# W4 and the two weights of the last layer as split operands in float32r, in a four-layer graph network on one core

## The chip, the cores and the metric

The kernel runs on one core of a Trainium2 chip. The metric is the device time of one execution in microseconds (us). Engines: TensorE (PE; PEld is its weight load), VectorE (DVE), ScalarE (ACT), GpSimd (POOL) and SyncE (SP, which issues most DMAs).

## The reference

128 nodes with 512 features, 4096 edges (src, dst) with 64 features each. Four layers follow each other, and after each x = layernorm(x + layer(x)):

```
L0: attention over the edges' adjacency, then a feed-forward part (not touched by the change)
L1: h   = mish([x[src], x[dst], edge_attr] @ W1 + b1)        # 4096 x 512
    agg = segment_sum(mish(h @ W2 + b2), dst)                # 128 x 512
    u   = mish([x, agg] @ W3 + b3)
    out = layernorm(x + u @ W4 + b4) * gamma + beta
L2: two graph convolutions, 512 -> 128 -> 512
L3: h   = x @ W_self.T + mean_of_neighbours(x) @ W_neigh.T + bias
    out = layernorm(h) * gamma + beta
```

## The kernel before

Everything is on chip after the first load. A float32 matmul of the source appears in the trace as two PE instructions (two passes), each with a weight load of its own; a float32r matmul is one. Where float32r is used, an operand v is split: hi = float32r(v), lo = v - hi, and the product is the sum of three matmuls, hi*hi + hi*lo + lo*hi. Before the change that holds for W1 and W2 of L1 and for the edge tensors; W3, W4 and all that comes after them are float32.

**The loop.** L1's edges go in G = 8 groups g of 512, each of 4 tiles t of 128. PE's order in group g is written out (lines 705 to 717): second_layer(g, 0), first_layer(g+1, 0), sum_messages(g-1), first_layer(g+1, 1), second_layer(g, 1), first_layer(g+1, 2 and 3), second_layer(g, 2 and 3). In the last group, g = 7, the first_layer parts are absent. sum_messages (671) adds the messages of tile t to bank 0 with two matmuls, from Mhi (678) and Mlo (679), and waits before each tile for `m_lo` of that tile. For each tile DVE adds the bias to the bank (z2_out, 994), ACT takes mish twice, to Mhi (380) and to M (381), and DVE subtracts (message_low, 999). DVE's order (1019 to 1041) and ACT's (388 to 400) are written out as well; each engine works in order, so an instruction put into either list delays all that stand after it. On DVE a group ends with one_hot (1006), z2_out 2, message_low 2, z2_out 3, message_low 3.

**The tail.** After the loop PE runs the last sum, W3 (update, 719; matmuls in line 472) and W4 (741, matmuls in line 463: banks 2 and 4 each take half of the 512 columns, K in four chunks c). ACT turns W3's banks into uT (404), DVE adds the residual (823) and normalises. PE then multiplies by ones (748), turns W_self and W_neigh by transposes (turn, 683, eight calls; ACT copies each out in line 408 to WsT, chunks 0 to 3, and WnT), transposes y (754; ACT copies xT in 415), and does L2: 760, DVE's r0 (1058, 1066), 767, ACT's r1g (418), 770, ACT's p1g (420), 776, and DVE's statistics (816) and norm (841). For L3 it transposes xs, forms the neighbours' mean (783, bank 2), and multiplies by WsT and WnT (788, 791), all in line 463. DVE copies xT (1075) and nmT (1077), adds beta (1079) and takes the statistics of banks 4 and 0 (1080).

**SP** loads W3, W4, W_self and W_neigh during the loop, each behind a count of finished second_layer tiles (246 to 253).

```
for t in ts:                                     # sum_messages, PE
    pe.wait_ge(S["m_lo"], GT * g + t + 1)
    mm(AGG[:, :], Dg[:, t, :], Mhi[:, t, :], start=g == 0 and t == 0, stop=False)
    done = mm(AGG[:, :], Dg[:, t, :], Mlo[:, t, :], start=False, stop=g == G - 1 and t == GT - 1)
```

Of the kernel before, what the change touches and what calls it, by code (L numbers as in the profile page):

```python
# [40 lines left out]
def gnn_kernel(nc, a, out):  # L41

    ctx = ExitStack()
    with ctx:
# [36 lines left out]
        def overlay(*spots):  # L81

            made = {}
            with ExitStack() as st:
                end = 0
                for name, place, units, dt in sorted(spots, key=lambda s: s[1]):
                    if place > end:
# [14 lines left out]
        low = overlay(("Clo", 0, 32, F32R), ("Mlo", 64, 4, F32R))  # L102
        last = overlay(("W3", 0, 8, F32), ("W4", 8, 4, F32), ("WsR", 12, 4, F32), ("WnR", 16, 4, F32),
                       ("WsT", 32, 4, F32), ("WnT", 36, 4, F32), ("uT", 40, 1, F32), ("aggT", 41, 1, F32), ("agg_sb", 42, 1, F32),
                       ("nmT", 43, 1, F32), ("xb_late", 44, 1, F32), ("r1g", 45, 1, F32), ("p1g", 46, 1, F32), ("r0", 47, 1, F32),
                       ("G1", 78, 1, F32), ("G2", 79, 1, F32))
        ctx.enter_context(nc.sbuf_tensor("region", [P, 95 * D], F32))

        def chunks(v, k):
            return v.rearrange("p (c n) -> p c n", c=k)  # L110
# [20 lines left out]
        W3, W4, WsR, WnR = chunks(last["W3"], 2 * KC), chunks(last["W4"], KC), chunks(last["WsR"], KC), chunks(last["WnR"], KC)  # L131
        WsT, WnT, uT, aggT, nmT = (chunks(last[n], KC) for n in ("WsT", "WnT", "uT", "aggT", "nmT"))
        G1, G2 = chunks(last["G1"], KC), last["G2"]
# [19 lines left out]
        def quarter(b, j):  # L153
            return b[:, P * j:P * (j + 1)]
# [19 lines left out]
        for name in ("x_in ids_in row_ids_in0 row_ids_in1 st_ready vecs_in ea_in wq_in0 wq_in1 wq_in2 wq_in3 wk_in0 wk_in1 wk_in2 wk_in3 ids_twice wv_in wo_in f1_in f2_in w1_in wc_in w2_in w3_in w4_in g_in ws_in wn_in b1g_in "  # L174
# [6 lines left out]
                     "agg_ready aggT_done aggT_ready u_done u_ready o_done "  # L181
                     "ones_ready sum_done sum_ready y2_ready y2T_done y2T_ready z_done r0_ready g1_done g1_ready g2_done g2_ready g3_done nm_done nm_ready l3_done wt_done wt_ready y_centred y_final0 y_final1 "
                     "dve_chain").split():
# [98 lines left out]
        def _(act):  # L282
# [93 lines left out]
            def message(g, t):  # L376
# [4 lines left out]
                act.activation(M[:, t, :], M[:, t, :], ACT.Mish).then_inc(S["m_hi"], 1)  # L381

            for j in range(KC):
                hidden(0, j)
# [3 lines left out]
            for g in range(G):  # L388
                ahead = 1 <= g < G - 1
                if ahead:  # L390
                    hidden(g + 1, 0)
                message(g, 0)
                if ahead:
                    hidden(g + 1, 1)
                message(g, 1)
                if ahead:
                    hidden(g + 1, 2)
                    hidden(g + 1, 3)
                message(g, 2)
                message(g, 3)  # L400

            for j in range(KC):
                act.wait_ge(S["u_done"], j // 2 + 1)
                bias_out(uT[:, j, :], quarter(bank[5 if j >= 2 else 7], j), "L1_gnn_b3", j, ACT.Mish).then_inc(S["u_ready"], 1)
            def turned_out(qs):
# [7 lines left out]
            for h in range(2):  # L413
                act.wait_ge(S["y2T_done"], h + 1)
                act.activation(half(flat(xT[:, :, :]), h), (bank[2], bank[4])[h][:, 0:D // 2], ACT.Copy).then_inc(S["y2T_ready"], 1)
            turned_out(range(TURNED_FIRST, 2 * KC))
            act.wait_ge(S["g1_done"], 1)
            act.activation(r1g, bank[3][:, 0:HID2], ACT.Relu).then_inc(S["g1_ready"], 1)
            act.wait_ge(S["g2_done"], 1)
            act.activation(p1g, bank[4][:, 0:N], ACT.Copy).then_inc(S["g2_ready"], 1)  # L420


# [9 lines left out]
        def _(pe):  # L432
# [303 lines left out]
            pe.wait_ge(S["w4_in"], 16)  # L736
            pe.wait_ge(S["z2_read"], GT * G)
            for h in range(2):
                pe.wait_ge(S["u_ready"], 2 * (h + 1))
                for b in range(2):  # L740
                    done = columns_by((bank[2], bank[4]), uT, W4, b, (2 * h, 2 * h + 1), 0, KC - 1)
                    if h == 1:
                        done.then_inc(S["o_done"], 1)
# [38 lines left out]
            for j in range(KC):  # L782
                done = mm(quarter(bank[2], j), xs[:, P * j:P * (j + 1)], Cn[:, :], start=True, stop=True)
            done.then_inc(S["nm_done"], 1)
            for h in range(2):
                pe.wait_ge(S["nT_ready"], 4 + h + 1)
                for b in range(2):
                    columns_by((bank[4], bank[0]), xT, WsT, b, (2 * h, 2 * h + 1), None, None)
            pe.wait_ge(S["nm_ready"], 1)
            for h in range(2):  # L790
                columns_by((bank[4], bank[0]), nmT, WnT, h, range(KC), None, KC - 1).then_inc(S["l3_done"], 1)


        @block.vector
        def _(dve):
# [205 lines left out]
            def one_hot(g):  # L1001

                if g >= 1:
# [3 lines left out]
                                iota_row[:, :].unsqueeze(1).to_broadcast([P, GT, N]), ALU.is_equal).then_inc(S["m_oh"], 1)  # L1007

            for j in range(KC):
                z1_out(0, j)  # L1010
# [8 lines left out]
            for g in range(G):  # L1019
                ahead = 1 <= g < G - 1  # L1020
                if ahead:
                    z1_out(g + 1, 0)
                z2_out(g, 0)
                if ahead:
                    z1_out(g + 1, 1)
                    hidden_low(g + 1, 0)
                message_low(g, 0)
                z2_out(g, 1)
                if ahead:
                    hidden_low(g + 1, 1)  # L1030
                    z1_out(g + 1, 2)
                    z1_out(g + 1, 3)
                message_low(g, 1)
                if ahead:
                    hidden_low(g + 1, 2)
                    hidden_low(g + 1, 3)
                one_hot(g)
                z2_out(g, 2)
                message_low(g, 2)
                z2_out(g, 3)  # L1040
                message_low(g, 3)
# [6 lines left out]
            chain(v.tensor_tensor(xb_late, xs[:, :], r("L1_gnn_beta"), ALU.add))  # L1048
            v.memset(ones, 1.0).then_inc(S["ones_ready"], 1)
            st = residual((bank[2], bank[4]), xw, S["o_done"])  # L1050
            norm_gain(y[:, :], y[:, :], r("L1_gnn_gamma"), xb_late, S["y2_ready"], st)
            dve.wait_ge(S["y2_ready"], 2)
            norms[0] += 1
            v.bn_aggr(mv[:, :], statistics(y[:, :])).then_inc(S["stat_ready"], 1)
            dve.wait_ge(S["stat_ready"], norms[0])
            dve.wait_ge(S["sum_ready"], 1)
# [10 lines left out]
            for h in range(2):  # L1067
                if h == 1:
                    chain(off_mean(1))
                v.scalar_tensor_tensor(out=half(xw, h), in0=half(xs, h), scalar=rstd[:, 0:1], in1=half(row["L2_gnn_b2"], h),  # L1070
                                       op0=ALU.mult, op1=ALU.add).then_inc(S["xw_ready"], 1)

            norm((bank[5], bank[6]), xs[:, :], S["nx_ready"], bank_statistics((bank[5], bank[6]), S["g3_done"]))

            out_halves(xT_flat, (bank[1], bank[3]), S["nT_done"], 4, S["nT_ready"])
            dve.wait_ge(S["nm_done"], 1)
            v.tensor_copy(flat(nmT), bank[2][:, :]).then_inc(S["nm_ready"], 1)
            dve.wait_ge(S["nx_ready"], 6)
# [28 lines left out]
```

## Time and profile before

| what | value |
|---|---|
| median of 3 runs | 244.72 us (244.4 to 245.69) |
| the profiled execution's own time | 245.73 us |
| its span, first to last instruction | 243.8 us |
| PE busy | 230.8 us, 95% of the span |
| DVE busy | 153.4 us, 63% |
| ACT busy | 120.6 us, 49% |
| mean granted clock of TensorE | 0.99 |

A line of the trace gives the line of the kernel, the engine, the operation, what is written from what, the shapes and the count. Matmuls are pipelined, so their durations overlap: what one costs in a row of them is the distance between starts. A granted clock of 1.00 is 2.4 GHz, 0.5 is 1.2 GHz.

### The profile page before, as it was taken

To read this page: it belongs to the slowest core of one execution; us is meant where nothing else is said; L and a number is where in the kernel's file an instruction comes from. 1 tells how busy PE (TensorE), PEld (TensorE's weight loads), DVE (VectorE), ACT (ScalarE), POOL (GpSimd) and SP (SyncE) were. 2 spreads that over 40 slices of the span, in tenths; PEclk is the share of its full clock that TensorE was granted. 3 is DMA by queue.
4 is the path that set the end of the run, shared out by engine and by line. 5 is a ranking of instruction groups with operands and counts; after the bars stand their busy time and mean duration, and the time that the engine had idled before them with its cause. 6 is when DMAs were issued, how large, how long until landed. Compare 5 with 4: busy or idle time off the path is not lost.

```text
span 243.8 us, 3226 instructions
## 1 busy us (share of the span) xinstructions
PE 230.8 (95%) x1231; PEld 185.9 (76%) x1231; DVE 153.4 (63%) x271; ACT 120.6 (49%) x220; POOL 6.8 (3%) x18
## 2 busy tenths in 40 slices
PE   7999999998999999999999999999999999997980
PEld 3977788765676787888888888888888889996760
DVE  3639785577579655875856848758558454363625
ACT  0326198747729834745735646457355343244000
POOL 0020000001000000000000000000000000000001
PEclk9999999999999999999999999999999999999995
DMA  6999979930690000009022050040000000000001
GB/s 208 307 400 386 397 249 383 356 137 0 163 255 15 0 0 0 3 8 330 5 100 76 0 172 1 9 166 0 0 0 3 0 0 0 3 0 0 3 0 44
DMA packets 12320, 25.48 MB, mean 105 GB/s; under 512 B 1017, under 2 KB 1937, under 8 KB 11921
## 3 DMA queue, kind: packets, MB, share of 16 engines
q1 hardware_dynamic: 11520, 24.78, 30.0%
q10 hardware_dynamic: 784, 0.50, 0.8%
q8 instruction: 10, 0.16, 0.3%
q14 instruction: 6, 0.04, 0.0%
HBM read 25.01 MB, written 0.26 MB: 104 GB/s over the span
## 4 chain that ended last, share of the span: by engine, by line
PE 86%; DVE 6%; ACT 3%; issue 2%; POOL 1%; POOLq 0%; DVEq 0%; ACTq 0%
PE bank L668 36%; PE bank L651 12%; PE bank L463 9%; PE bank L472 6%; PE bank L519 4%; PE bank L535 3%; PE bank L678 3%; PE bank L679 3%; PE bank L482 2%; PE bank L446 1%; ACT WsT L408 1%; PE bank L630 1%; DVE y L884 1%; PE bank L631 1%; PE bank L635 1%
## 5 line engine op out<-in xcount | busy, mean ns | idle before, releaser
L668 PE MATMUL bank<-W2hi,Hhi 128*128 128x512 f32 x128 | 49.8, 389 | 0.0
L668 PE MATMUL bank<-W2hi,Clo 128*128 128x512 f32 x128 | 49.8, 389 | 0.0
L668 PE MATMUL bank<-W2lo,Hhi 128*128 128x512 f32 x128 | 49.8, 389 | 0.0
L380 ACT ACTIVATE Mhi<-M 128x512 fp32r<-128x512 f32 x32 | 20.2, 632 | 45.4 <-DVE M L994 45.4
L999 DVE TENSOR_TENSOR Mlo<-M,Mhi 128x512 fp32r<-128x512 f32 x32 | 22.1, 690 | 24.4 <-ACT M L381 24.4
L994 DVE TENSOR_TENSOR M<-bank,b2r 128x512 f32<-128x512 f32 x32 | 22.0, 687 | 12.6 <-PE bank L679 7.6
L668 PEld LDWEIGHTS bank<-W2hi,Clo 128*128 128x128 f32 x128 | 24.0, 188 | 5.0
L668 PEld LDWEIGHTS bank<-W2hi,Hhi 128*128 128x128 f32 x128 | 24.0, 188 | 5.0
L668 PEld LDWEIGHTS bank<-W2lo,Hhi 128*128 128x128 f32 x128 | 24.0, 188 | 5.0
L373 ACT ACTIVATE Hhi<-C 128x512 fp32r<-128x512 f32 x32 | 20.0, 625 | 12.4 <-DVE C L980 12.1
L293 ACT ACTIVATE C<-bank,cols 128x512 f32<-128x512 f32 x32 | 19.9, 685 | 11.6 <-PE bank L519 11.5
L980 DVE TENSOR_TENSOR C<-bank,C 128x512 f32<-128x512 f32 x32 | 21.4, 690 | 5.1 <-PE bank L651 4.1
L985 DVE TENSOR_TENSOR Clo<-C,Hhi 128x512 fp32r<-128x512 f32 x32 | 22.0, 688 | 3.7 <-ACT C L374 3.6
L651 PE MATMUL bank<-ST,AB 128*128 128x512 f32 x64 | 20.0, 399 | 0.0
L374 ACT ACTIVATE C<-C 128x512 f32<-128x512 f32 x32 | 19.8, 618 | 0.0
L381 ACT ACTIVATE M<-M 128x512 f32<-128x512 f32 x32 | 19.7, 616 | 0.0
L651 PE MATMUL bank<-DT,AB 128*128 128x512 f32 x64 | 19.4, 390 | 0.0
L651 PEld LDWEIGHTS bank<-ST,AB 128*128 128x128 f32 x64 | 11.6, 188 | 3.9 <-DVE C L980 1.0
L651 PEld LDWEIGHTS bank<-DT,AB 128*128 128x128 f32 x64 | 12.0, 188 | 2.6
L678 PE MATMUL bank<-Mhi,Dg 128*128 128x512 f32 x32 | 12.6, 395 | 0.0
L679 PE MATMUL bank<-Mlo,Dg 128*128 128x512 f32 x32 | 12.5, 389 | 0.0
L271 POOL TENSOR_TENSOR rstd<-mv,mhalf 128x1 f32<-128x1 f32 x8 | 4.4, 550 | 207.4 <-DVE mv L846 194.6
(193 smaller groups left out, 314.6 us busy)
## 6 DMA issues: line engine op xcount, KB each, us to landing
F<-in_L_gnn_W SPq DMA_DIRECT2D x2, 2048.0 KB, 14.3
W1raw<-in_L_gnn_W SPq DMA_DIRECT2D x1, 2048.0 KB, 22.5
ids<-in_src SPq DMA_DIRECT2D x2, 1024.0 KB, 14.0
W<-in_L_gnn_W SPq DMA_DIRECT2D x1, 2048.0 KB, 8.6
Wq<-in_L_gnn_Wq SPq DMA_DIRECT2D x4, 256.0 KB, 4.5
Wk<-in_L_gnn_Wk SPq DMA_DIRECT2D x4, 256.0 KB, 7.0
Wv<-in_L_gnn_Wv SPq DMA_DIRECT2D x1, 1024.0 KB, 10.1
ea<-in_edge_attr SPq DMA_DIRECT2D x1, 1024.0 KB, 11.8
```

What stands on the lines that cost most here:

```text
L293: return act.activation(dst, src, func, bias=cols[:, col[name] + j:col[name] + j + 1])
L373: act.activation(Hhi[:, g % 2, j, :], C[:, g, j, :], ACT.Mish)
L380: act.activation(Mhi[:, t, :], M[:, t, :], ACT.Mish)
L463: done = mm(banks[h][:, 0:D // 2], lhs[:, c, :], rhs[:, c, D // 2 * h:D // 2 * (h + 1)], start=c == start, stop=c == stop)
L651: done = mm(ST1[u % 3][:, :], w[:, P * j:P * (j + 1)], x[:, GE * g:GE * (g + 1)], start=k == 0, stop=k == len(terms) - 1)
L668: done = mm(ST2[t][:, :], x[:, c, e], w[:, c, :], start=c == 0 and i == 0, stop=c == KC - 1 and i == 2)
L678: mm(AGG[:, :], Dg[:, t, :], Mhi[:, t, :], start=g == 0 and t == 0, stop=False)
L679: done = mm(AGG[:, :], Dg[:, t, :], Mlo[:, t, :], start=False, stop=g == G - 1 and t == GT - 1)
L980: v.tensor_tensor(C[:, g, j, :], ST1[u % 3][:, :], C[:, g, j, :], ALU.add).then_inc(S["z1_read"], 1)
L985: v.tensor_tensor(Hlo[:, g, j, :], C[:, g, j, :], Hhi[:, g % 2, j, :].bitcast(F32), ALU.subtract).then_inc(S["h_lo"], 1)
L994: v.tensor_tensor(M[:, t, :], ST2[t][:, :], row["L1_gnn_b2"], ALU.add).then_inc(S["z2_read"], 1)
L999: v.tensor_tensor(Mlo[:, t, :], M[:, t, :], Mhi[:, t, :].bitcast(F32), ALU.subtract).then_inc(S["m_lo"], 1)
```

## The change

W4, W_self and W_neigh, and the operands that meet them (u, x and the neighbours' mean), are split in hi and lo as above, and their matmuls, 256 columns each, are done in three float32r terms. ACT makes the hi part of W4 in group 5 (one chunk after each message), DVE its lo part in group 6, two chunks after one_hot and two after message_low 2. ACT and DVE make the parts of W_self and W_neigh in the tail, at the places shown. The lo parts lie where the whole operands lay, or beside them. ACT takes mish twice from each bank of W3. The diff, without the overlay's places and the names:

```diff
+            def w4_high(g, c):
+                if g == G - 3:
+                    act.wait_ge(S["w4_in"], 16)
+                    act.activation(W4hi[:, c, :], W4[:, c, :], ACT.Copy).then_inc(S["w4_hi"], 1)
...
                 message(g, 0)
+                w4_high(g, 0)
...
                 message(g, 1)
+                w4_high(g, 1)
...
                 message(g, 2)
+                w4_high(g, 2)
                 message(g, 3)
+                w4_high(g, 3)
-            for j in range(KC):
-                act.wait_ge(S["u_done"], j // 2 + 1)
-                bias_out(uT[:, j, :], quarter(bank[5 if j >= 2 else 7], j), "L1_gnn_b3", j, ACT.Mish).then_inc(S["u_ready"], 1)
+            for h in range(2):
+                act.wait_ge(S["u_done"], h + 1)
+                for dst, signal in ((uThi, "u_hi"), (uT, "u_ready")):
+                    for j in (2 * h, 2 * h + 1):
+                        bias_out(dst[:, j, :], quarter(bank[5 if h else 7], j), "L1_gnn_b3", j, ACT.Mish).then_inc(S[signal], 1)
+
+            def ws_high(c):
+                act.wait_ge(S["wt_ready"], c + 1)
+                act.activation(WsThi[:, c, :], WsT[:, c, :], ACT.Copy).then_inc(S["ws_hi"], 1)
...
                 act.activation(half(flat(xT[:, :, :]), h), (bank[2], bank[4])[h][:, 0:D // 2], ACT.Copy).then_inc(S["y2T_ready"], 1)
+            ws_high(0)
+            ws_high(1)
             turned_out(range(TURNED_FIRST, 2 * KC))
             act.wait_ge(S["g1_done"], 1)
             act.activation(r1g, bank[3][:, 0:HID2], ACT.Relu).then_inc(S["g1_ready"], 1)
+            ws_high(2)
             act.wait_ge(S["g2_done"], 1)
             act.activation(p1g, bank[4][:, 0:N], ACT.Copy).then_inc(S["g2_ready"], 1)
+            ws_high(3)
+            act.wait_ge(S["wt_ready"], 2 * KC)
+            for c in range(KC):
+                act.activation(WnThi[:, c, :], WnT[:, c, :], ACT.Copy).then_inc(S["wn_hi"], 1)
+            for h in range(2):
+                act.wait_ge(S["nT_done"], 4 + h + 1)
+                act.activation(half(flat(xThi), h), (bank[1], bank[3])[h][:, 0:D // 2], ACT.Copy).then_inc(S["xl_hi"], 1)
+            act.wait_ge(S["nm_done"], 1)
+            act.activation(flat(nmThi), bank[2][:, :], ACT.Copy).then_inc(S["nm_hi"], 1)
...
+            pe.wait_ge(S["w4_lo"], KC)
             for h in range(2):
-                pe.wait_ge(S["u_ready"], 2 * (h + 1))
+                cs = (2 * h, 2 * h + 1)
+                pe.wait_ge(S["u_hi"], 2 * (h + 1))
                 for b in range(2):
-                    done = columns_by((bank[2], bank[4]), uT, W4, b, (2 * h, 2 * h + 1), 0, KC - 1)
+                    columns_by((bank[2], bank[4]), uThi, W4hi, b, cs, 0, None)
+                    columns_by((bank[2], bank[4]), uThi, W4lo, b, cs, None, None)
+                pe.wait_ge(S["u_lo"], h + 1)
+                for b in range(2):
+                    done = columns_by((bank[2], bank[4]), uTlo, W4hi, b, cs, None, KC - 1)
...
+            out_banks = (bank[4], bank[0])
+            pe.wait_ge(S["ws_hi"], KC)
             for h in range(2):
-                pe.wait_ge(S["nT_ready"], 4 + h + 1)
+                pe.wait_ge(S["xl_hi"], h + 1)
                 for b in range(2):
-                    columns_by((bank[4], bank[0]), xT, WsT, b, (2 * h, 2 * h + 1), None, None)
-            pe.wait_ge(S["nm_ready"], 1)
-            for h in range(2):
-                columns_by((bank[4], bank[0]), nmT, WnT, h, range(KC), None, KC - 1).then_inc(S["l3_done"], 1)
+                    columns_by(out_banks, xThi, WsThi, b, (2 * h, 2 * h + 1), None, None)
+            for h in range(2):
+                pe.wait_ge(S["xl_lo"], h + 1)
+                for b in range(2):
+                    columns_by(out_banks, xTlo, WsThi, b, (2 * h, 2 * h + 1), None, None)
+            pe.wait_ge(S["ws_lo"], KC)
+            for b in range(2):
+                columns_by(out_banks, xThi, WsTlo, b, range(KC), None, None)
+            pe.wait_ge(S["wn_hi"], KC)
+            pe.wait_ge(S["nm_hi"], 1)
+            for b in range(2):
+                columns_by(out_banks, nmThi, WnThi, b, range(KC), None, None)
+            pe.wait_ge(S["nm_lo"], 1)
+            pe.wait_ge(S["wn_lo"], KC)
+            for b in range(2):
+                columns_by(out_banks, nmTlo, WnThi, b, range(KC), None, None)
+                columns_by(out_banks, nmThi, WnTlo, b, range(KC), None, KC - 1).then_inc(S["l3_done"], 1)
...
+            def weight_low(lo, whole, hi, cs, name):
+                for c in cs:
+                    dve.wait_ge(S[f"{name}_hi"], c + 1)
+                    v.tensor_tensor(lo[:, c, :], whole[:, c, :], hi[:, c, :].bitcast(F32), ALU.subtract).then_inc(S[f"{name}_lo"], 1)
...
                 one_hot(g)
+                if g == G - 2:
+                    weight_low(W4lo, W4, W4hi, (0, 1), "w4")
                 z2_out(g, 2)
                 message_low(g, 2)
+                if g == G - 2:
+                    weight_low(W4lo, W4, W4hi, (2, 3), "w4")
                 z2_out(g, 3)
                 message_low(g, 3)
...
             v.memset(ones, 1.0).then_inc(S["ones_ready"], 1)
+            for h in range(2):
+                dve.wait_ge(S["u_hi"], 2 * (h + 1))
+                dve.wait_ge(S["u_ready"], 2 * (h + 1))
+                v.tensor_tensor(half(flat(uTlo), h), half(flat(uT), h), half(flat(uThi), h).bitcast(F32), ALU.subtract).then_inc(S["u_lo"], 1)
             st = residual((bank[2], bank[4]), xw, S["o_done"])
...
             v.bn_aggr(mv[:, :], statistics(y[:, :])).then_inc(S["stat_ready"], 1)
+            weight_low(WsTlo, WsT, WsThi, (0, 1), "ws")
             dve.wait_ge(S["stat_ready"], norms[0])
             dve.wait_ge(S["sum_ready"], 1)
             dve.wait_ge(S["z_done"], 1)
...
+            weight_low(WsTlo, WsT, WsThi, (2, 3), "ws")
             norm((bank[5], bank[6]), xs[:, :], S["nx_ready"], bank_statistics((bank[5], bank[6]), S["g3_done"]))
 
-            out_halves(xT_flat, (bank[1], bank[3]), S["nT_done"], 4, S["nT_ready"])
-            dve.wait_ge(S["nm_done"], 1)
-            v.tensor_copy(flat(nmT), bank[2][:, :]).then_inc(S["nm_ready"], 1)
+            for h in range(2):
+                dve.wait_ge(S["xl_hi"], h + 1)
+                v.tensor_tensor(half(flat(xTlo), h), (bank[1], bank[3])[h][:, 0:D // 2], half(flat(xThi), h).bitcast(F32),
+                                ALU.subtract).then_inc(S["xl_lo"], 1)
+            dve.wait_ge(S["nm_hi"], 1)
+            v.tensor_tensor(flat(nmTlo), bank[2][:, :], flat(nmThi).bitcast(F32), ALU.subtract).then_inc(S["nm_lo"], 1)
+            weight_low(WnTlo, WnT, WnThi, range(KC), "wn")
             dve.wait_ge(S["nx_ready"], 6)
```

## Rows read from the trace of the kernel before

**Rows 1.** The page: busy time, then two groups: busy us, mean ns | idle before

```profile
PE 230.8 (95%) x1231; PEld 185.9 (76%) x1231; DVE 153.4 (63%) x271; ACT 120.6 (49%) x220; POOL 6.8 (3%) x18
...
L380 ACT ACTIVATE Mhi<-M 128x512 fp32r<-128x512 f32 x32 | 20.2, 632 | 45.4 <-DVE M L994 45.4
...
L668 PEld LDWEIGHTS bank<-W2hi,Clo 128*128 128x128 f32 x128 | 24.0, 188 | 5.0
```

**Rows 2.** The chain in order of time, 190 us on: start, length, what

```profile
194.41 8.16 PE bank L668 x36
...
208.49 3.84 PE bank L472 x32
212.32 3.46 PE bank L463 x16
...
229.77 6.92 PE bank L463 x32
```

**Rows 3.** Issue of W4's load by SP, by tile (its start is the 124.6)

```profile
L249 SPq DMA_DIRECT2D W<-in_L_gnn_W x1: 378/378/378, 124.6 to 124.6; - x1
```

**Rows 4.** ACT in the timeline, group 6: start, length, line, what

```profile
188.75 0.63 ACT L380 ACTIVATE Mhi<-M 128x512 fp32r<-128x512 f32 x1 [1.96 <-DVE M L994]
189.29 0.62 ACT L381 ACTIVATE M<-M 128x512 f32<-128x512 f32 x1
```

**Rows 5.** DVE in the timeline, group 6

```profile
188.03 0.68 DVE L994 TENSOR_TENSOR M<-bank,b2r 128x512 f32<-128x512 f32 x1
189.94 0.69 DVE L999 TENSOR_TENSOR Mlo<-M,Mhi 128x512 fp32r<-128x512 f32 x1 [1.22 <-ACT M L381]
190.55 0.68 DVE L994 TENSOR_TENSOR M<-bank,b2r 128x512 f32<-128x512 f32 x1
192.45 0.69 DVE L999 TENSOR_TENSOR Mlo<-M,Mhi 128x512 fp32r<-128x512 f32 x1 [1.22 <-ACT M L381]
```

**Rows 6.** PE in the timeline: the last tile's Mhi matmul of group 6

```profile
193.80 0.39 PE L678 MATMUL bank<-Mhi,Dg 128*128 128x512 f32 x1
```

**Rows 7.** The timeline of the tail, from W3's second half to L3's statistics

```profile
208.49 3.84 PE L472 MATMUL bank<-aggT,W 128*128 128x128 f32 x32
...
212.16 3.62 PE L463 MATMUL bank<-W,uT 128*128 128x256 f32 x16
212.36 0.63 ACT L293 ACTIVATE uT<-bank,cols 128x128 f32<-128x128 f32 x2 [1.16 <-PE bank L472]
214.95 0.42 DVE L823 TENSOR_TENSOR y<-bank,xw 128x256 f32<-128x256 f32 x1 [5.67 <-PE bank L463]
...
215.89 0.42 DVE L823 TENSOR_TENSOR y<-bank,xw 128x256 f32<-128x256 f32 x1
...
217.15 2.07 ACT L408 ACTIVATE WsT<-bank 128x512 f32<-128x512 f32 x4 [0.16 <-PE bank L689]
...
219.55 0.70 ACT L415 ACTIVATE xT<-bank 128x256 f32<-128x256 f32 x2
...
221.66 0.35 DVE L1058 SCALAR_TENSOR_TENSOR r<-r,mv,bank 128x128 f32<-128x128 f32 x1 [1.92 <-PE bank L760]
...
223.30 0.28 ACT L418 ACTIVATE r1g<-bank 128x128 f32<-128x128 f32 x1 [0.22 <-PE bank L767]
...
224.22 0.28 ACT L420 ACTIVATE p1g<-bank 128x128 f32<-128x128 f32 x1 [0.64 <-PE bank L770]
...
225.52 0.93 DVE L816 BATCH_NORM_STATS2 stats<-bank 128x6 f32<-128x256 f32 x2 [1.62 <-PE bank L776]
...
229.81 0.69 DVE L1077 COPY nmT<-bank 128x512 f32<-128x512 f32 x1 [0.47 <-PE bank L783]
...
236.79 0.43 DVE L816 BATCH_NORM_STATS2 stats<-bank 128x6 f32<-128x256 f32 x1 [1.29 <-PE bank L463]
```

**Rows 8.** A window of the tail: length, busy us by engine, granted clock

```profile
220.00:224.00 4.00, 2.99 (x22) 2.67 (x23) 2.13 (x6) 2.11 (x5) 0.37 (x1) 1.00 0.00 0
```

More of the change, by code:

```diff
@@ L102, in gnn_kernel @@
         low = overlay(("Clo", 0, 32, F32R), ("Mlo", 64, 4, F32R))
[L103 to L106, printed above, removed]
+        last = overlay(("W3", 0, 8, F32), ("W4", 8, 4, F32), ("WsR", 12, 4, F32), ("WnR", 16, 4, F32), ("WsThi", 20, 4, F32R),
+                       ("WnThi", 24, 4, F32R), ("xThi", 28, 1, F32R), ("xTlo", 29, 1, F32R), ("nmThi", 30, 1, F32R),
+                       ("nmTlo", 31, 1, F32R), ("WsT", 32, 4, F32), ("WnT", 36, 4, F32), ("uT", 40, 1, F32), ("aggT", 41, 1, F32),
+                       ("agg_sb", 42, 1, F32), ("uThi", 43, 1, F32R), ("xb_late", 44, 1, F32), ("r1g", 45, 1, F32), ("p1g", 46, 1, F32),
+                       ("r0", 47, 1, F32), ("G1", 78, 1, F32), ("G2", 79, 1, F32), ("W4hi", 91, 4, F32R))
+        rest = overlay(("W4lo", 8, 4, F32R), ("WsTlo", 32, 4, F32R), ("WnTlo", 36, 4, F32R), ("uTlo", 40, 1, F32R))
         ctx.enter_context(nc.sbuf_tensor("region", [P, 95 * D], F32))
@@ L131, in gnn_kernel @@
         W3, W4, WsR, WnR = chunks(last["W3"], 2 * KC), chunks(last["W4"], KC), chunks(last["WsR"], KC), chunks(last["WnR"], KC)
-        WsT, WnT, uT, aggT, nmT = (chunks(last[n], KC) for n in ("WsT", "WnT", "uT", "aggT", "nmT"))
+        WsT, WnT, uT, aggT = (chunks(last[n], KC) for n in ("WsT", "WnT", "uT", "aggT"))
+        W4hi, WsThi, WnThi, xThi, xTlo, nmThi, nmTlo, uThi = (chunks(last[n], KC) for n in (
+            "W4hi", "WsThi", "WnThi", "xThi", "xTlo", "nmThi", "nmTlo", "uThi"))
+        W4lo, WsTlo, WnTlo, uTlo = (chunks(rest[n], KC) for n in ("W4lo", "WsTlo", "WnTlo", "uTlo"))
         G1, G2 = chunks(last["G1"], KC), last["G2"]
@@ L181, in gnn_kernel @@
                      "agg_ready aggT_done aggT_ready u_done u_ready o_done "
-                     "ones_ready sum_done sum_ready y2_ready y2T_done y2T_ready z_done r0_ready g1_done g1_ready g2_done g2_ready g3_done nm_done nm_ready l3_done wt_done wt_ready y_centred y_final0 y_final1 "
+                     "ones_ready sum_done sum_ready y2_ready y2T_done y2T_ready z_done r0_ready g1_done g1_ready g2_done g2_ready g3_done nm_done l3_done w4_hi w4_lo u_hi u_lo ws_hi ws_lo wn_hi wn_lo xl_hi xl_lo nm_hi nm_lo wt_done wt_ready y_centred y_final0 y_final1 "
                      "dve_chain").split():
```

## The prediction

> **What bounds the kernel now.** I read the page first: PE is busy 95% of the span, DVE 63%, ACT 49% [rows 1]. The chain in order of time then says where PE sets the end. In the loop it is an unbroken row of PE pieces, such as 36 matmuls of second_layer in 8.16 us, 227 ns each (512 columns, float32r) [rows 2]. So what PE loses or gains in the loop is lost or gained in the whole. In the tail the chain changes engines: PE for W3 and W4, then ACT, PE and DVE by turns through L2, then PE for L3's two weights, then DVE. The places that matter are the two stretches of line 463, 16 passes in 3.46 us for W4 and 32 in 6.92 us for W_self and W_neigh [rows 2]: 216 ns a pass. These are what the change makes shorter. The timeline of ACT and DVE in the loop and in the tail gives the covers and slacks.
>
> **1. The price of a float32r matmul of 256 columns.** The trace has none. From 512 columns at 227 ns, half is 113 ns. The 128-column passes of line 472, each with a weight load, run 32 in 3.84 us, 120 ns with the restart in it [rows 2], so a load per 120 ns is sustained, although one load alone is shown as 188 ns [rows 1]. Ends: 113 and 188 ns (loads that don't overlap). I take 113, since the row at 120 ns shows loads of the same size overlapping. W4 then has 24 matmuls in 2.72 us for 3.46, L3 48 in 5.44 us for 6.92. PE alone would gain 0.74 + 1.48 = 2.2 us.
>
> **2. W4hi on ACT, group 5.** Four copies of 128x512; ACT starts the next such instruction 0.54 us after one [rows 4]. Each stands behind a message. ACT idles 45.4 us before the 32 Mhi, 1.4 us each time [rows 1], so each copy lies in such a gap, or pushes a pair of hidden activations by 0.5 us that the next gap takes up. Cost 0; if that cover were gone, up to 4 x 0.54 = 2.2 us. W4's load is issued at 124.6 us [rows 3], forty before the first copy; the SP queue is unchanged.
>
> **3. W4lo on DVE, group 6: the part that costs.** DVE starts back-to-back operations of this size 0.61 us apart (189.94 to 190.55) [rows 5]. The first two subtractions go between one_hot and z2_out 2, which has been free to run (it starts at 188.03 right behind one_hot, with no wait shown). So z2_out 2 moves from 188.03 to 189.25. What hangs on it is a chain: ACT's mish 0.72 later, message_low 2 at 1.91 after z2_out [rows 4, 5]. That moves to 191.15. The other two subtractions come before z2_out 3, which moves from 190.55 to 192.98; message_low 3 comes 1.90 later, at 194.87 instead of 192.45, and ends at 195.56 [rows 5]. Behind it waits PE: the Mhi matmul of that tile started at 193.80 [rows 6], 0.66 after the old end of 193.14. So the four subtractions, 2.42 us, meet a slack of 0.66: PE stands for 1.8 us. A restart costs a little: 32 passes from 208.49 reach the next start at 212.16 [rows 7], 3.67 us where 32 at 111 would be 3.55, so 0.1. I take **+1.9 us**. In order behind the wait stand all of group 7 and the tail, and PE had no pause there to take it up. In group 7 the z2_outs depend on PE's own results and shift with it. Ends: 0, if PE finds slack that I don't see, and 2.5, if every subtraction costs its full 0.69 instead of 0.61 and the restart 0.3.
>
> The row shows 690 ns for one operation and 0.61 between starts. The Trainium skill (VectorE: DVE Perf Modes, The TRN2 errata) gives a float32 tensor_tensor (N+151)/0.96, 691 ns at 512; the duration agrees, and taken as the price of each in a row it would make this step 2.2 instead of 1.9. The starts decide.
>
> **4. W4 itself.** In old times (loop loss aside): PE is free at 212.32. uThi comes first from ACT, at the old time of uT (second half 212.36 + 0.63 = 212.99 [rows 7]); its terms are needed at 213.7. uT's second pair ends at 213.53, uTlo half a microsecond later, 214.0; needed at 214.6. So PE runs through and ends at 215.04 instead of 215.78. But DVE's residual is two halves of two operations each: y half 0 at 214.95, half 1 at 215.89, only just behind its bank [rows 2, 7]. Now bank 2's last matmul is the 22nd of 24, at 212.32 + 2.49 = 214.81 against 12 of 16 passes, 214.91. DVE's chain to y gains **0.1** only. PE's matmul by ones, the turns and ACT's copies (217.15) come 0.7 earlier. ACT's xT (219.55) was late by ACT's own queue; it can now start at 218.85, as the transposes of y allow.
>
> **5. The splitting of W_self in L2.** ACT: ws_high 0 and 1 stand behind xT, which ends 0.7 earlier, at 219.4 by starts; they are ready at 220.0 and 220.6. DVE: two subtractions, at 220.05 and 220.65, before r0's first step (1058), which can start at 221.3; it started at 221.66 behind PE's line 760 [rows 7], which now ends 0.7 earlier. So the two waits cost nothing against before, they eat half of the 0.7; a gain of 0.35 is left there. If it were not for that head start they would cost 0.7. ws_high 2 fits between r1g (223.30) and p1g (224.22), 0.92 apart [rows 7], 0.28 + 0.54 taken. ws_high 3 follows p1g, and DVE subtracts chunk 3 at about 224.8 to 225.4, with line 816 behind it: that started at 225.52 [rows 7], could have started at 225.17, and now does at 225.42. Left: **-0.1**. Ends: -0.5 and +0.7. Behind p1g ACT has only the four WnThi, 2.2 us, done by 227 and needed at 232.
>
> **6. L3.** Before: PE from 229.77 for 6.92 us, and the second statistics at 236.79 [rows 2, 7]. Now PE does 32 matmuls (W_self's three terms, nmThi) in 3.6 us, to 233.4; xThi by ACT and xTlo by DVE (0.43 each half) are done before their terms come up. The rest waits for DVE. nm is in its bank at 229.8 [rows 7]; ACT copies, 0.63; nmTlo starts at 230.5, then four subtractions of W_neigh from 231.1, 0.61 apart, the last ending at 233.6. PE stands 0.2 and restarts, 16 matmuls take 1.8, end at 235.6; the statistics at 235.75 instead of 236.79. Part **-1.0**. The gain of 1.5 is cut by DVE. DVE's addition of beta (0.68) goes behind the subtractions, still ahead of the bank. Ends: -1.5 (no wait) and +2.1 (188 ns: 48 x 0.188 = 9.0).
>
> **The sum.** +1.9 - 0.1 - 1.0 = +0.8 us. (Step 4's 0.1 is within the 0.1 left after step 5.) Against the profiled execution: 245.73 us with a span of 243.8, so 246.5 us with a span of 244.6. It was 1.0 above the median of the runs shown; applied to the median, 244.72 + 0.8 = **245.5 us**. A measurement of this kernel can tell about 0.5%, 1.2 us, from no change.
>
> **The rivals.**
> - **No stall in group 6.** If the message chain had room, or PE recovered it, steps 4 to 6 stand alone: -1.1, 243.6 us; without step 6's wait -1.6. Against it: slack of 0.66 for 2.42 us of added work in an in-order queue, and a chain with no pause in it. Chance 0.08, faster only at its far end.
> - **Weight loads bind at 256 columns** (the other side: clearly slower). Each of the 72 matmuls brings a load. At 188 ns [rows 1] W4 takes 4.5 us (+1.05) and L3 9.0 us (+2.1, with DVE's wait hidden behind it): +1.9 + 1.05 + 2.1 - 0.1 = +5.0, 249.7 us. It passes the +1.2 mark from about 120 ns on. Against it: the 120 ns row. For it: that row is two-pass float32, and no float32r loads stand closer than 227. Chance 0.10.
> - **The W_self waits on DVE take the place of PE's.** If ACT doesn't reach xT early (its copies, not the turns, hold the line), r0 moves by 0.7 and line 816 by 0.3 more: +0.8 + 1.0 = +1.8, 246.5 us. The point is whether ACT's first copy out (217.15) moves with the end of W4. I think so, as PE's ones follow W4 directly. Chance 0.12.
> - **The clock.** The window 220 to 224 has PE busy 2.99 of 4 us at a granted clock of 1.00, 2.4 GHz [rows 8]; PE's pauses in the change are of that kind, the longest 1.8 us. If the clock fell to its level of 1.2 GHz after the stall, group 7's 36 matmuls of 227 ns alone would cost 8.2 more: 253 us. The Trainium skill (TensorE: Matmul & The Clock Gate, HAM oscillation) warns of idle gaps in a matmul stream; no row here shows a fall in the tail. Chance 0.03.
> - **The change doesn't shorten matmuls at all**, if 256 columns cost 216 ns in float32r as in a float32 pass: 24 and 48 at 216 are 5.2 and 10.4 us: +1.9 + 1.7 + 3.5 - 0.1 = +7.0, 251.7. Chance 0.02.
>
> **How the numbers follow.** The forecast has 0.65. Its own spread comes from step 3 (1.6 to 2.2 as starts or durations rule), step 5 (-0.5 to +0.3) and step 6 (-1.3 to -0.7): 244.7 to 246.2, with a tenth of its weight over +1.2. Faster by over 0.5%: 0.04, half of the no-stall case. Slower by over 0.5%: 0.07 of the forecast, 0.10 for loads, 0.12 for the waits, 0.05 for clock and no saving, less what stays inside: 0.31. Same 0.65. The range takes in the no-stall case, down to 243.6, and the waits' case with the loads' near half, up to 247.2.
>
> **What would show it.** Right: PE idle about 1.8 us before the last pair of lines 678 and 679 of group 6, released by DVE's Mlo; a DVE row of W4lo x4 with starts 0.6 apart; starts of line 463's matmuls 113 ns apart; DVE's line 1058 0.3 earlier against the end of the loop; PE waiting 0.2 to 0.4 for DVE's WnTlo in L3. Wrong: no idle there; line 463's starts over 130 ns apart; a PE wait on ACT's W4hi or before r0 longer than now; a granted clock under 0.95 after group 6.

## The result and the profile after

The changed kernel takes 246.31 us (median of 20 runs) and the kernel before 245.14 (20 runs): ratio 1.0047, 95% interval 1.0037 to 1.0057, so 0.9 to 1.4 us slower. The forecast was 245.5 us, 0.8 above the median then known. The profiled execution has a span of 244.6 us, as the sum had it, and a time of 246.63. Of the six executions of e10 below, one took 385.23 us at a mean granted clock of 0.559, where the other five took 243.1 to 244.26 at 0.992 to 0.994; its time and its ratio leave that one out, and no trace shows what happened in it.

From the page of the changed kernel, its busy line:

```profile
PE 230.0 (94%) x1255; PEld 185.7 (76%) x1255; DVE 161.0 (66%) x285; ACT 129.2 (53%) x239; POOL 6.8 (3%) x18
```

PE lost 0.8 us of work and DVE gained 7.6, ACT 8.6 [rows 1]. The span is nevertheless longer. The waits of PE, longest first, name the place (in the new numbering 712 and 713 are the two sums, 1055 message_low, 1050 z2_out, 1062 one_hot, 1068 all weight subtractions, 497 the 256-column matmuls, 506 those of W3):

```profile
PE bank L516 <- DVE ident L924: 1.7, 1, 1.7
PE bank L712 <- DVE Mlo L1055: 1.6, 1, 1.6
```

The first stands at the start of both kernels; the second is new. DVE in group 6, and PE at group 6's last sum:

```profile
187.19 0.68 DVE L1062 TENSOR_TENSOR Dg<-dcol,iota_row 128x512 fp32r<-128x512 int32 x1
187.79 1.29 DVE L1068 TENSOR_TENSOR W4lo<-W,W4hi 128x512 fp32r<-128x512 f32 x2
188.99 0.69 DVE L1050 TENSOR_TENSOR M<-bank,b2r 128x512 f32<-128x512 f32 x1
190.90 0.69 DVE L1055 TENSOR_TENSOR Mlo<-M,Mhi 128x512 fp32r<-128x512 f32 x1 [1.22 <-ACT M L387]
191.51 1.28 DVE L1068 TENSOR_TENSOR W4lo<-W,W4hi 128x512 fp32r<-128x512 f32 x2
192.71 0.68 DVE L1050 TENSOR_TENSOR M<-bank,b2r 128x512 f32<-128x512 f32 x1
194.61 0.69 DVE L1055 TENSOR_TENSOR Mlo<-M,Mhi 128x512 fp32r<-128x512 f32 x1 [1.22 <-ACT M L387]
...
193.32 0.39 PE L713 MATMUL bank<-Mlo,Dg 128*128 128x512 f32 x1
195.36 0.50 PE L712 MATMUL bank<-Mhi,Dg 128*128 128x512 f32 x1 [1.64 <-DVE Mlo L1055]
195.69 0.39 PE L713 MATMUL bank<-Mlo,Dg 128*128 128x512 f32 x1
```

and one_hot of the same group in the kernel before:

```profile
187.43 0.68 DVE L1006 TENSOR_TENSOR Dg<-dcol,iota_row 128x512 fp32r<-128x512 int32 x1
```

One_hot to the last message_low took 5.02 us before (187.43 to 192.45 [rows 5]) and takes 7.42 now, 2.40 more for four subtractions. PE stands 1.64 us ahead of the last tile's sum. From the matmul in front of it, that sum starts 2.04 us later (193.32 to 195.36) where a start follows the last one by 0.23, so it is 1.81 late; the next start comes 0.33 behind it and not 0.23, which is the restart. This execution was 0.24 us ahead of the old one at one_hot, and 195.36 against 193.80 [rows 6] gives the same 1.8.

The tail in the chain in order of time, start, length, what:

```profile
210.19 3.84 PE bank L506 x32
214.03 2.88 PE bank L497 x24
...
221.43 0.53 ACT WsThi L425
...
221.98 0.81 DVE WsTlo L1068 x2
...
223.19 0.35 DVE r L1128
...
226.57 0.69 DVE WsTlo L1068
...
231.39 3.83 PE bank L497 x32
235.22 0.08 issue
235.30 2.16 PE bank L497 x16
...
237.55 0.44 DVE stats L872
```

The start of W3's second half (208.49 before [rows 2], 210.19 now) serves as a mark: what the change does in the tail comes behind it. From it to the last statistics, the tail took 28.30 us before (to 236.79 [rows 7]) and takes 27.36 now. So the tail gains 0.94, and the loop loses 1.70 + 0.24 = 1.94, the 1.81 and the restart. Together +1.0 us, inside the measured interval. W4 is 0.58 us shorter on PE (3.46 to 2.88), L3 goes from 6.92 to 6.07 with a short wait in it, and links of W_self's splitting stand in the chain twice: ahead of r0, where PE's line 760 stood, and ahead of L2's statistics (226.57), where PE's lines 773 and 776 stood.

### The profile page after: what moved, and what is told of

The parts are those of the page before. It is cut to its first block, busy times and chain, and to the rows that moved or that the text cites. A ratio compares the mean times of both kernels' runs of the same rounds, so it can differ in the third digit from the quotient of the medians.

```text
span 244.6 us, 3313 instructions
## 1 busy us (share of the span) xinstructions
PE 230.0 (94%) x1255; PEld 185.7 (76%) x1255; DVE 161.0 (66%) x285; ACT 129.2 (53%) x239; POOL 6.8 (3%) x18
## 4 chain that ended last, share of the span: by engine, by line
PE 83%; DVE 7%; ACT 4%; issue 3%; POOL 1%; POOLq 0%; DVEq 0%; ACTq 0%
PE bank L702 32%; PE bank L685 12%; PE bank L497 8%; PE bank L506 6%; PE bank L553 4%; PE bank L569 3%; PE bank L712 3%; PE bank L713 3%; PE bank L516 2%; PE bank L486 1%; DVE W4lo L1068 1%; PE bank L480 1%; ACT WsT L430 1%; PE bank L664 1%; PE bank L588 1%
```

## The experiments

All ratios are to runs of the kernel before made together with them. "Tail" is the distance from the start of W3's second half to the start of the last statistics in the chain.

| kernel | ratio (interval) | PE's pause ahead of group 6's last sum | tail, us |
|---|---|---|---|
| before | 1 | none | 28.30 |
| changed | 1.0047 (1.0037 to 1.0057) | 1.64 | 27.36 |
| e1: W4lo in group 7's waits | 0.9970 (0.9956 to 0.9984) | none | 27.35 |
| e2: two in group 6, two in group 7 | 0.9992 (0.9979 to 1.0006) | 0.44 | 27.35 |
| e3: last layer alone | 0.9982 (0.9969 to 0.9995) | none | 27.86 |
| e4: W4 alone, W4lo in group 7 | 0.9982 (0.9971 to 0.9993) | none | 27.77 |
| e7: e1 and one W_self subtraction before r0 | 0.9957 (0.9943 to 0.9972) | none | 27.00 |
| e8: e1 and one W_neigh subtraction in GpSimd's wait | 0.9962 (0.9948 to 0.9975) | none | 27.34 |
| e9: e7 and e8 | 0.9955 (0.9939 to 0.9971) | none | 27.01 |
| e10: e7 and two W_neigh subtractions in ACT's waits | 0.9926 (0.9902 to 0.9949) | none | 26.70 |

The mark itself moves by up to a microsecond between single profiles (208.53 in e1, 207.62 in e8, with the same loop), so the tail is read from the traces and the whole from the ratios. That scatter lies ahead of group 6. From group 6's one_hot to the mark it is 21.06 us before (187.43 to 208.49), 21.05 in e1, 21.78 in e2 and 23.00 in the changed kernel: a loss of 0, 0.72 and 1.94 us.

**e1: the four W4lo subtractions where DVE waits for ACT.**

```diff
                 z2_out(g, 0)
...
+                if g == G - 1:
+                    weight_low(W4lo, W4, W4hi, (0,), "w4")
                 message_low(g, 0)
...
                 one_hot(g)
-                if g == G - 2:
-                    weight_low(W4lo, W4, W4hi, (0, 1), "w4")
                 z2_out(g, 2)
```

and the same for chunks 1 to 3 ahead of message_low 1 to 3; group 6's lines for chunks 2 and 3 are out as well.

> The changed kernel, with DVE's four W4lo subtractions moved from group 6 to group 7, one between z2_out and message_low of each tile, where DVE waits 1.22 us for ACT and one subtraction takes 0.61. Theory (group 6's stall is the whole loss): PE's pause of 1.64 us before group 6's last tile is gone, no other pause in the loop, the rest of the change as before, so 1.9 us under the changed kernel and about 0.8 us under the kernel before, ratio 0.997. Rival (the subtractions cost wherever DVE does them): the pause comes back in group 7, before the last sums, and the ratio stays near 1.005.

Measured: 244.33 us against 245.25, ratio 0.9970. DVE in group 7, in the timeline of e1:

```profile
194.57 0.69 DVE L1050 TENSOR_TENSOR M<-bank,b2r 128x512 f32<-128x512 f32 x1 [1.39 <-PE bank L713]
195.18 0.68 DVE L1068 TENSOR_TENSOR W4lo<-W,W4hi 128x512 fp32r<-128x512 f32 x1
196.48 0.69 DVE L1055 TENSOR_TENSOR Mlo<-M,Mhi 128x512 fp32r<-128x512 f32 x1 [0.62 <-ACT M L387]
```

The message_low comes 1.91 us after its z2_out, as it did without a subtraction between them [rows 5]: its wait for ACT is 0.62 instead of 1.22, and the subtraction took the difference. From 62 us to the end of the loop PE has no wait. So the order, not the amount, of DVE's work cost 1.9 us; from the changed kernel to this one the ratio falls by 0.0077, which is 1.9 us.

**e2: half the dose.**

```diff
                 one_hot(g)
                 if g == G - 2:
                     weight_low(W4lo, W4, W4hi, (0, 1), "w4")
                 z2_out(g, 2)
                 message_low(g, 2)
-                if g == G - 2:
-                    weight_low(W4lo, W4, W4hi, (2, 3), "w4")
                 z2_out(g, 3)
```

with chunks 2 and 3 ahead of message_low 1 and 2 of group 7.

> The changed kernel with two of the four W4lo subtractions left in group 6 (behind one_hot) and two in group 7's waits. Theory of a fixed slack: two subtractions are 1.21 us against a slack of 0.66, so PE pauses 0.4 to 0.55 us before group 6's last tile, and the kernel is 1.2 to 1.4 us under the changed one, ratio to before 0.999 to 1.000. Rival (each subtraction costs its share of the stall, 0.48 us): 0.95 us under the changed kernel, pause 0.9 us, ratio 1.001.

The row of e2 in PE's timeline:

```profile
193.59 0.50 PE L712 MATMUL bank<-Mhi,Dg 128*128 128x512 f32 x1 [0.44 <-DVE Mlo L1055]
```

No subtraction gives no pause, two give 0.44 us, four give 1.64. The last two cost 1.20, their full 0.60 each. The first two cost 0.44 by this count, for 1.21 us of work. (The profile counts idle time from the modelled end of the matmul before; by starts the sum is 0.17 later than that, 0.61 and 1.81 us, which is the added 1.21 and 2.40 less 0.60 both times.) That is a fixed slack of 0.60; a share per subtraction (0.9 us here) is out.

**e3: the last layer alone.** W4's part undone:

```diff
-                pe.wait_ge(S["u_hi"], 2 * (h + 1))
+                pe.wait_ge(S["u_ready"], 2 * (h + 1))
                 for b in range(2):
-                    columns_by((bank[2], bank[4]), uThi, W4hi, b, cs, 0, None)
-                    columns_by((bank[2], bank[4]), uThi, W4lo, b, cs, None, None)
-                pe.wait_ge(S["u_lo"], h + 1)
-                for b in range(2):
-                    done = columns_by((bank[2], bank[4]), uTlo, W4hi, b, cs, None, KC - 1)
+                    done = columns_by((bank[2], bank[4]), uT, W4, b, (2 * h, 2 * h + 1), 0, KC - 1)
```

> Only the last layer's two weights in split operands; W4 in float32 as before, no W4hi, W4lo, uThi, uTlo. Theory (the W_self subtractions before r0 are covered only by the head start that W4's shorter matmuls give ACT): without the head start r0's first step comes 0.4 us later than before, the statistics of L2 0.5 us later, L3 saves 0.86, so 0.35 us under the kernel before, ratio 0.9985. Rival (those waits are free anyway): r0 not later, 0.9 us under before, ratio 0.9965.

**e4: W4 alone**, with W4lo as in e1 and the last layer as before the change (ws_high, WnThi, xThi, nmThi and their subtractions left out, lines 788 and 791 of before put back).

> Only W4 in split operands, its W4lo in group 7's waits; the last layer in float32 as before. Theory: PE's W4 takes 2.88 us for 3.46 and no pause comes in the loop; y gains nothing (DVE-bound), but ACT's copies and xT come 0.57 earlier, and as r0 waited on PE's line 760 behind them, the whole is 0.5 us under before, ratio 0.998. Rival (DVE's chain to y sets the end, the head start is lost): same as before, ratio 1.000.

Both came to 0.9982. L2's second statistics in the chain of before, then e3's chain, then e4's timeline:

```profile
226.02 0.44 DVE stats L816
```

```profile
207.60 3.84 PE bank L500 x32
...
221.12 0.35 DVE r L1108
...
225.56 0.44 DVE stats L860
...
235.46 0.44 DVE stats L860
```

```profile
207.69 3.84 PE L491 MATMUL bank<-aggT,W 128*128 128x128 f32 x32
...
218.17 0.75 ACT L436 ACTIVATE xT<-bank 128x256 f32<-128x256 f32 x2
...
220.33 0.35 DVE L1101 SCALAR_TENSOR_TENSOR r<-r,mv,bank 128x128 f32<-128x128 f32 x1 [1.36 <-PE bank L785]
```

r0's first step after the mark: 13.17 us before (221.66 - 208.49 [rows 7]), 13.52 in e3, 12.64 in e4, 13.00 in the changed kernel. W4's shorter matmuls bring it 0.53 forward, W_self's two subtractions put it 0.35 back, and the second number is the same with W4's head start (13.00 - 12.64 = 0.36) and without it (13.52 - 13.17 = 0.35). L3 itself then gains 0.87 in e3: 9.90 us between the two statistics against 10.77 before (236.79 [rows 7] less 226.02). The two tails' gains, 0.44 and 0.53, add to 0.97; the changed kernel has 0.94. So the two parts of the change add up without disturbing each other.

**e5 and e6: the price of a float32r matmul by its width.** The changed kernel with W4 in 48 matmuls of 128 columns, and in 12 of 512:

```diff
+                def narrow(lhs, rhs, b, start, stop):
+                    for c in cs:
+                        for k in range(2):
+                            done = mm(quarter((bank[2], bank[4])[b], k), lhs[:, c, :], rhs[:, c, P * (2 * b + k):P * (2 * b + k + 1)],
+                                      start=c == start and k == 0, stop=c == stop and k == 1)
+                    return done
...
-                    columns_by((bank[2], bank[4]), uThi, W4hi, b, cs, 0, None)
...
+                    narrow(uThi, W4hi, b, 0, None)
```

```diff
+                def wide(lhs, rhs, start, stop):
+                    for c in cs:
+                        done = mm(bank[2][:, :], lhs[:, c, :], rhs[:, c, :], start=c == start, stop=c == stop)
+                    return done
...
-                    columns_by((bank[2], bank[4]), uThi, W4hi, b, cs, 0, None)
...
+                wide(uThi, W4hi, 0, None)
```

and the other two terms in the same way; in e6 the residual reads both halves from bank 2.

> The changed kernel with W4 in 48 matmuls of 128 columns. Theory A (a fixed 13 ns per float32r matmul, weight loads fast enough): 53 + 13 = 67 ns each, 3.2 us for W4, the time 0.3 to 0.5 us over the changed kernel. Theory B (a weight load of this size takes at least 107 to 120 ns of PE's time, and two do not overlap more than that): 5.2 to 5.8 us for W4, the time 2 to 2.9 us over the changed kernel.

> The changed kernel with W4 in 12 matmuls of 512 columns instead of 24 of 256, all in one bank. 256 columns cost 120 ns where half of the 512-column price is 113. Theory A (a fixed 13 ns per float32r matmul over its columns at 2.4 GHz: 213 + 13 = 227, 107 + 13 = 120): 12 take 2.72 us, as in the loop. Theory B (the weight load binds at 120 ns, and 227 is a limit of another kind): 2.72 us as well; so this one sizes the gain of 0.16 us on PE, and the time stays within 0.3 us of the changed kernel, as the residual's first half must now wait for all of W4.

The rows of W4 in the chains of e5 and of e6:

```profile
213.24 5.31 PE bank L779 x48
```

```profile
214.03 2.77 PE bank L778 x12
```

| columns | columns at 2.4 GHz, ns | measured per matmul, ns |
|---|---|---|
| 512 (the loop, 36 in 8.16 us [rows 2]) | 213 | 227 |
| 512 (e6) | 213 | 231 |
| 256 (24 in 2.88) | 107 | 120 |
| 128 (48 in 5.31) | 53 | 111 |

At 512 and 256 columns the price is the columns and 13 ns (e6's 12 also hold the 0.04 us of their start). At 128 columns it would be 67 by that count and is 111: there something that does not shrink with the columns binds, as theory B had it for the loads. So 256 columns lie just above that floor, and cutting the float32r terms to 128 columns only costs. The two were run once each: 248.18 us (before, also once: 245.66) and 246.64 (before: 245.24). Their tails say more: e5's is 29.78, 2.42 longer than the changed kernel's, as theory B had it, and e6's 27.45, 0.09 longer, since the residual starts later by 0.11. That what binds at 128 columns is the load was not shown: no run changes the load alone.

**e7: one subtraction before r0.**

```diff
-            weight_low(WsTlo, WsT, WsThi, (0, 1), "ws")
+            weight_low(WsTlo, WsT, WsThi, (0,), "ws")
...
-            weight_low(WsTlo, WsT, WsThi, (2, 3), "ws")
+            weight_low(WsTlo, WsT, WsThi, (1, 2, 3), "ws")
```

> The kernel of the first experiment (W4lo in group 7) with one W_self subtraction before r0 instead of two; the other three stand behind xw, ahead of L2's statistics. In the two traces that have them, r0's first step comes 0.35 us later with the two subtractions than without (13.00 after 12.64 us from W3's second half, 13.52 after 13.17), and the first of them ends before PE's z. Theory: only the second one costs; r0 0.35 us earlier, L2's statistics 0.3 to 0.4 earlier, the whole 0.35 us under the first experiment, ratio to before 0.9955. Rival: three subtractions do not fit between xw and the statistics (2.7 do by my count, and the last waits for ACT), so the gain is given back there: ratio 0.997.

In the timeline of e7:

```profile
208.37 3.84 PE L506 MATMUL bank<-aggT,W 128*128 128x128 f32 x32
...
220.15 0.69 DVE L1068 TENSOR_TENSOR WsTlo<-WsT,WsThi 128x512 fp32r<-128x512 f32 x1 [0.49 <-ACT WsThi L425]
...
221.01 0.35 DVE L1132 SCALAR_TENSOR_TENSOR r<-r,mv,bank 128x128 f32<-128x128 f32 x1 [0.17 <-PE bank L800]
...
223.16 1.92 DVE L1068 TENSOR_TENSOR WsTlo<-WsT,WsThi 128x512 fp32r<-128x512 f32 x3
225.00 0.89 DVE L872 BATCH_NORM_STATS2 stats<-bank 128x6 f32<-128x256 f32 x2
```

r0 comes 12.64 after the mark, as in e4 without any subtraction, and waits 0.17 for PE. The three others fit. The tail is 0.35 shorter, as expected.

**e8: a W_neigh subtraction while DVE waits for GpSimd's rstd.** In L2's norm, between the aggregate and the wait:

```diff
                 v.bn_aggr(mv[:, :], statistics(src) if st is None else st).then_inc(S["stat_ready"], 1)
+                if meanwhile is not None:
+                    meanwhile()
                 dve.wait_ge(S["rstd_ready"], norms[0])
...
-            norm((bank[5], bank[6]), xs[:, :], S["nx_ready"], bank_statistics((bank[5], bank[6]), S["g3_done"]))
+            norm((bank[5], bank[6]), xs[:, :], S["nx_ready"], bank_statistics((bank[5], bank[6]), S["g3_done"]),
+                 lambda: weight_low(WnTlo, WnT, WnThi, (0,), "wn"))
...
-            weight_low(WnTlo, WnT, WnThi, range(KC), "wn")
+            weight_low(WnTlo, WnT, WnThi, range(1, KC), "wn")
```

> The kernel of the first experiment with the first W_neigh subtraction moved from L3 to DVE's 0.66 us wait for GpSimd's rstd in L2's norm. Theory (DVE sets the last 16 matmuls of L3): PE's wait there goes, 48 matmuls at 120 ns run through in 5.76 us for 6.07, so 0.3 us under the first experiment, ratio 0.9958. Rival (the subtraction delays the norm by what it saves later): ratio 0.997, and the norm's first half starts 0.1 us or more later behind the statistics.

The mechanism that was expected came, 48 matmuls in one piece, and so did the rival. From e8's chain:

```profile
225.51 0.25 DVE mv L895
225.76 0.07 issue
225.83 0.88 POOL rstd L277
226.71 0.03 issue
226.73 0.56 DVE xs L899
...
229.11 5.76 PE bank L497 x48
```

and the subtraction beside it, in DVE's timeline:

```profile
225.67 0.63 DVE L1070 TENSOR_TENSOR WnTlo<-WnT,WnThi 128x512 fp32r<-128x512 f32 x1
```

The norm starts 1.22 us behind the aggregate; in e1 it is 0.90 (226.44 to 227.34). The 0.31 that L3 gained is lost there: tail 27.34. The ratio, 0.9962, is no proof of a gain beside e1's 0.9970. **e9**, with e7's edit as well, tells the same.

> All three moves in one kernel. Theory: the gains add, 0.35 + 0.3 = 0.65 us under the first experiment, about 243.7 us, ratio to before 0.9943. Rival (they meet at the same engine: DVE has no more room): no better than the better of the two, ratio 0.9955.

0.9955 and a tail of 27.01, e7's 27.00: the gains did not add, not for want of room on DVE but for GpSimd's longer operation.

**e10: the same work in waits for ACT.** e7, and in L3:

```diff
+            weight_low(WnTlo, WnT, WnThi, (0,), "wn")
             for h in range(2):
                 dve.wait_ge(S["xl_hi"], h + 1)
...
                                 ALU.subtract).then_inc(S["xl_lo"], 1)
+            weight_low(WnTlo, WnT, WnThi, (1,), "wn")
             dve.wait_ge(S["nm_hi"], 1)
             v.tensor_tensor(flat(nmTlo), bank[2][:, :], flat(nmThi).bitcast(F32), ALU.subtract).then_inc(S["nm_lo"], 1)
-            weight_low(WnTlo, WnT, WnThi, range(KC), "wn")
+            weight_low(WnTlo, WnT, WnThi, (2, 3), "wn")
```

> The kernel with W4lo in group 7 and one W_self subtraction before r0 (ratio 0.9957), and two of the W_neigh subtractions moved into DVE's waits for ACT in L3: chunk 0 behind the norm, where DVE waits 0.50 us for xThi, and chunk 1 between xTlo and nmTlo, where it waits 0.68. In the run with a subtraction in GpSimd's wait, PE ran 48 matmuls through in 5.76 us, but GpSimd's rstd took 0.87 us for 0.55 beside it and gave the gain back. Theory (it was GpSimd's slow operation that took it back, and in a wait for ACT nothing slows): 5.76 us in L3, no operation of GpSimd longer than 0.55 us, from W3's second half to the last statistics 26.7 us for 27.0, ratio 0.9945. Rival (any DVE work there delays the chain to L3's first matmuls): 27.0 us, ratio 0.9957.

From e10's chain:

```profile
208.13 3.84 PE bank L506 x32
...
226.01 0.56 POOL rstd L277
...
228.98 5.76 PE bank L497 x48
...
234.83 0.44 DVE stats L872
```

Tail 26.70, as expected, rstd at its 0.55, L3's 48 matmuls in one piece. 243.63 us (median of five) against 245.41, ratio 0.9926 (0.9902 to 0.9949): this version beats both kernels. Its trace accounts for 1.6 us, 0.9935. Beside e7's 0.9957 the ratio alone is no proof, as the intervals overlap; the 0.30 us between the two tails is read from the traces.

## Why the prediction was right

The three terms of the sum came out at +1.94, -0.08 and -0.86 where +1.9, -0.1 and -1.0 were forecast: +1.0 for +0.8. The mechanism was right, and e1 and e2 show its main step. About the number some things are luck or need a word. The median, 246.31, lies 0.8 above the forecast 245.5; 0.42 of that is that the first three runs of the kernel before had a median of 244.72 and all 20 have 245.14. That 246.31 lies next to the 246.5 of the W_self rival is chance: its mechanism did not come. And the span of 244.6 agrees to the tenth only because this execution was 0.24 us ahead before the change acted. The rise of 0.47% also lies just under the 0.5% that the prediction drew between "same" and "slower", and the interval reaches over it; against the prediction's remark that 1.2 us can hardly be told from no change, 20 runs on each side do tell it.

- **Step 3, the loss in group 6.** Worked out: 2.42 us of work, slack 0.66, pause 1.8 with the restart 0.1, +1.9. Measured: 2.40, slack 0.60, a pause of 1.64 by the profile's count (the sum starts 1.81 late), +1.94 at the mark with the restart. e1 takes it away whole, e2 shows the slack. Its count by starts (0.61) and not by durations (0.69) was the right one: four W4lo take 0.60 each.
- **Step 1, the price of a matmul.** It was mis-sized: 113 ns by halving 227, measured 120. Halving also halved a fixed part of 13 ns. It made PE's own time 0.17 us too short at W4 and 0.34 at L3. Little of that reached the sum, which is luck: the 0.17 made r0 late (step 5), and of the 0.34 in L3 0.23 fall on the first 32 matmuls, whose end is covered by DVE's subtractions.
- **Step 4.** PE's W4 gained 0.58 for 0.74. DVE's y gained nothing: its first half is 6.52 us behind the mark against 6.46 before (214.95 - 208.49 [rows 7]), where 0.1 was expected. ACT's xT came 0.57 earlier against the mark, 0.7 was expected.
- **Step 5.** The end was right, -0.08 at the start of L3's matmuls for -0.1. The way to it was not: r0 came 0.17 us earlier against the mark (13.00 for 13.17), where 0.35 was expected, and the split of W_self's last chunk took back 0.10 (p1g still was 0.18 earlier, 15.55 for 15.73) where 0.25 was expected. Two misses cancelled. "If it were not for that head start they would cost 0.7" fell: e3 and e4 show that the two subtractions cost 0.35 with and without the head start, as ACT's xT, its WsThi and PE's line 760 all move with it. e7 shows that the second one was the whole cost.
- **Step 6.** -0.86 for -1.0. PE waits as forecast. From DVE's and the weight loads' timeline:

```profile
232.66 2.49 DVE L1068 TENSOR_TENSOR WnTlo<-WnT,WnThi 128x512 fp32r<-128x512 f32 x4
...
235.27 0.53 PEld L497 LDWEIGHTS bank<-WnThi,nmTlo 128*128 128x128 f32 x4 [0.26 <-issue]
```

  The profile puts the idle 0.26 to "issue", but the load starts 0.12 behind the end of the fourth subtraction (235.15), and with one or two subtractions fewer there (e8, e10) it is gone. The missing 0.14 lies in the price of the matmuls behind it: the last 16 took 2.16 us with the restart, not 1.8 and 0.1.
- **Step 2.** ACT's four W4hi cost nothing: PE has no wait in group 5, and the trace shows each copy in ACT's gap or a hidden pair pushed by one copy.

**The rivals.** No stall: out. Loads at 188 ns: out, though the 111 measured at 128 columns stands close below the 120. No saving, 216 ns: out, 120 was measured. W_self's waits: out in size (+1.0 was its price; r0 moved forward). The clock: out (its price, by the rival's own 245.5 and 8.2, is 253.7 and not 253). The window with the pause, from the changed kernel,

```profile
192.00:196.00 4.00, 2.36 (x11) 1.66 (x10) 2.08 (x4) 1.15 (x2) 0.00 (x0) 1.00 0.00 0
```

has PE busy 2.36 of 4 us at a granted clock of 1.00, and the starts from 195.69 to 198.91 behind the pause are 230 ns apart on average, where the kernel before has 227. So the pause brought no fall. The measured rise, 1.17 us at the medians, is above the 0.8 of the forecast and the 1.0 of the two traces; the interval reaches down to 0.9, and a difference of 0.2 us between them stays open.

## What to carry to other kernels

Before giving an in-order engine extra work, read what it waits for at that place: the same four subtractions cost 1.9 us in front of operations that were ready, and nothing where the engine waits 1.2 us for another one between two operations of a chain. Add up the whole delay along the chain and compare it with the one slack at its end; the first piece may be free and each further one costs its full length. And a shorter matmul stream helps only as far as its consumer's own queue and the splits feeding it allow: of the 1.74 us that PE's streams became shorter (0.58 at W4, 6.92 to 5.76 in L3), the tail gained 0.94.

## What the runs showed of the hardware

A float32r matmul with a 128-column load of its own costs its columns at 2.4 GHz and 13 ns more, at 512 (227) and at 256 columns (120); at 128 columns it costs 111 (e5). The Trainium skill (TensorE: Matmul & The Clock Gate, LDWEIGHTS) gives a load as its columns over 1.2 GHz, 107 ns for 128; the 111 of e5 fits it as a floor. No run here separates the load from other per-instruction costs. The Trainium skill (TensorE: Matmul & The Clock Gate, Back-to-back issue gap) has 2.5 ns over the columns for a matmul alone, and for a stream of pairs of load and matmul 81 ns at 128 columns and 131 at 512. The 111 and 227 of these float32r rows are above both, and the measurement decides.

GpSimd's operation on one column took 0.87 us instead of 0.55 when DVE's subtraction of two SBUF operands had begun 0.16 us ahead of it (e8, e9). The Trainium skill (SBUF — State Buffer, Who interferes with whom) says that a DVE instruction with two SBUF inputs contends with a GpSimd instruction that reads SBUF, and e8 agrees. In e7 a subtraction that began 0.41 us behind such a GpSimd operation left it at 0.55 and took its own 0.69. But the changed kernel has a pair in e8's order, DVE first, that did not slow:

```profile
218.82 0.77 DVE L911 SCALAR_TENSOR_TENSOR y<-y,mv,rows 128x512 f32<-128x512 f32 x1
218.86 0.55 POOL L277 TENSOR_TENSOR rstd<-mv,mhalf 128x1 f32<-128x1 f32 x1 [157.92 <-DVE mv L902]
```

Here DVE reads two SBUF operands too and began 0.04 us ahead. What sets the two cases apart was not tried.
